# Gathered rows in three buffers and one byte per edge in a two-part graph network on one Trainium2 core

## What is computed

```
h = relu(layernorm(x))
W = einsum('rb,bio->rio', w_comp, weight)             # 16 types from 8 bases
x = x + segment_sum((h @ W[type])[src], dst) + h_bias
h = relu(layernorm(x))
h = leaky(h @ enc_w + enc_b)                          # slope 0.1
for l in range(2):
    agg = segment_sum(h[src], dst) / max(degree, 1)
    h = leaky(agg @ lin_l_w[l] + lin_l_b[l] + h @ lin_r_w[l])
x = x + h
```

## Time and profile before

| | |
|---|---|
| median of 3 runs | 3645.25 us (3639.75 to 3645.88) |
| the profiled execution | 3647.71 us, its span 3645.6 us |
| busy: PE, DVE, ACT, POOL | 66%, 82%, 52%, 68% of the span |
| setup, relational, node, layer 1 main, late | 128.7, 1102.8, 1079.8, 705.6, 628.7 us |
| share of the DMA engines in these | 0.72, 0.66, 0.90, 0.97, 0.99 |

### The profile page before, as it was taken

The page is one execution under the profiler, slowest core; times in us unless marked ns, Lnnn a source line. Parts: engine busy times, 40 slices in busy tenths (PEclk is TensorE's granted clock), DMA queues, the critical chain, the costliest instruction groups (busy, mean ns, idle before and its releaser), DMA issues. The chain is left out here.

```text
span 3645.6 us, 58608 instructions
## 1 busy us (share of the span) xinstructions
PE 2416.4 (66%) x13938; PEld 1765.4 (48%) x13938; DVE 3003.8 (82%) x8321; ACT 1899.4 (52%) x4979; POOL 2486.9 (68%) x2363
## 2 busy tenths in 40 slices
PE   0669999999999588888888888478777780000000
PEld 0435555555555366666666666377777770000000
DVE  2569999999999699999999999688898884555665
ACT  0346666666666588888888888255454550000000
POOL 0257777777777577777777777666666645676665
PEclk9989999999999899999999999799999995555555
DMA  8776667666664599999999997599999988999998
GB/s 252 295 267 194 201 208 209 208 210 211 210 202 129 194 280 281 289 287 291 290 292 290 292 295 233 201 376 380 387 389 387 379 333 347 416 416 416 415 413 329
DMA packets 664350, 1065.77 MB, mean 292 GB/s; under 512 B 74065, under 2 KB 379651, under 8 KB 657586
## 3 DMA queue, kind: packets, MB, share of 16 engines
q1 hardware_dynamic: 486572, 599.67, 50.3%
q10 hardware_dynamic: 95904, 305.70, 21.0%
q0 software_dynamic: 81536, 156.64, 13.2%
HBM read 596.92 MB, written 488.74 MB: 298 GB/s over the span
## 5 line engine op out<-in xcount | busy, mean ns | idle before, releaser
L946 PE MATMUL y_ps_rel<-w_basis,ht_rel 128*128 128x512 f32 x1568 | 754.1, 604 | 56.0 <-DVE two_rel L815 55.7
L1694 POOL DMA_INDIRECT gat_l<-base_and_means,src_c x392 | 459.0, 1171 | 211.5 <-DVE act_gat_l L1801 107.4
L1699 POOL DMA_INDIRECT means<-late_l,put_c x392 | 418.0, 1066 | 232.1 <-issue 114.4
L1084 POOL DMA_INDIRECT base_and_means<-rows_node,odd_c x392 | 423.7, 1081 | 146.3 <-issue 122.7
L668 POOL DMA_INDIRECT gat_rel<-in_x_dram,src_c x392 | 401.3, 1024 | 157.3 <-issue 81.7
L1244 ACT ACTIVATE h_node<-base_node,shift_node,rstd_node 128x128 f32<-128x128 f32 x1176 | 500.4, 483 | 1.6 <-DVE shift_node L1334 1.6
L677 POOL DMA_INDIRECT agg<-rows_rel,put_c x392 | 401.8, 1025 | 134.2 <-issue 99.9
L1075 POOL DMA_INDIRECT term_node<-agg,src_c x392 | 380.8, 971 | 128.0 <-issue 118.9
L815 DVE SCALAR_TENSOR_TENSOR two_rel<-y_ps_rel,coef,two_rel 128x128 f32<-128x128 f32 x1568 | 438.0, 341 | 0.0
L946 PEld LDWEIGHTS y_ps_rel<-w_basis,ht_rel 128*128 128x128 f32 x1568 | 265.7, 192 | 266.9 <-issue 171.2
L1624 DVE TENSOR_TENSOR last_z_l<-last_z_l,node_done_l 128x1024 f32<-128x1024 f32 x98 | 120.2, 1227 | 268.3 <-DMA node_done_l<-means 268.3
(11 more groups left out here) (167 smaller groups left out, 5993.2 us busy)
## 6 DMA issues: line engine op xcount, KB each, us to landing
pairs_l<-base_and_means SPq DMA_DIRECT2D x196, 512.0 KB, 7.7
base_and_means<-zero_row SPq DMA_DIRECT2D x49, 1024.0 KB
means<-zero_row SPq DMA_DIRECT2D x49, 1024.0 KB
first_node<-in_x_dram SPq DMA_DIRECT2D x196, 256.0 KB
term_node<-agg SPq DMA_DIRECT2D x196, 256.0 KB
x<-base_node SPq DMA_DIRECT2D x196, 256.0 KB
base_and_means<-done_node SPq DMA_DIRECT2D x196, 256.0 KB
z<-node_done_l ACTq DMA_DIRECT2D x196, 256.0 KB, 7.3
```

Of the source, the lines that this page charges most:

```text
L946: nc.tensor.matmul(y_ps[(q + j) % 2][:, c * 512:(c + 1) * 512], ht[:, q, j, :], w_basis[:, 4 * c:4 * c + 4, :], start=True, stop=True).the ...
L1084: nc.gpsimd.indirect_dma_start(pair.rearrange("n (k f) -> (n k) f", k=2), bass.IndirectOffsetOnAxis(ap=odd_c[:, t:t + 1], axis=0), rows[:, ...
L1694: nc.gpsimd.indirect_dma_start(gat[:, q, j, :], None, source, bass.IndirectOffsetOnAxis(ap=src_c[:, t:t + 1], axis=0)).then_inc(s_gathered ...
L1699: nc.gpsimd.indirect_dma_start(means1, bass.IndirectOffsetOnAxis(ap=put_c[:, t:t + 1], axis=0), rows_, None, bounds_check=N - 1, oob_is_er ...
```

## The change

1. **One byte per edge.** The setup makes `run`: for each edge 0 if its run began before its tile, else one more than its place in the tile (1 to 128). It is stored as one byte per edge in `run_d` and turned into the column `run_c`. Every pass broadcasts 896 (512) bytes into `run_b` instead of 897 (513) floats into `dst_b`: a quarter of the bytes. `select` compares `run_b` with `run_c`; `find_open` compares `run_b` with the constant 0, so it becomes a TENSOR_SCALAR with one tensor in place of a TENSOR_TENSOR with two. The setup gains one POOL iota, four DVE steps on 128x512, a fifth set of four transposes and its copy, and one store.
2. **Three buffers.** `gat` of layer 1 has RING = 3 slots, with one semaphore each; the gather of half-step m waits for the adding up of m - 3.
3. **One tile later.** In layer 1 `carry_on` is done for the tile before the present one, `to_rows` three tiles behind instead of two, `finish` four instead of three.
4. `count_needed` stands behind the first `select` and `find_open`.

```diff
+                    link(nc.vector.tensor_copy(begins[:], begins_i[:]))
+                    link(nc.vector.tensor_tensor(after_begin[:], firsts[:], begins[:], ALU.subtract))
+                    link(nc.vector.tensor_scalar(run[:], after_begin[:], 0.0, None, ALU.max))
+                    nc.vector.tensor_copy(run_b[:], run[:]).then_inc(s_run, 1)
...
-                    for k, a in enumerate(order):
+                    for k, a in enumerate(order + [run]):
+                        if k == 4:
+                            pe.wait_ge(s_run, 1)
+                            pe.wait_ge(s_col, 1)
...
-                            sp.dma_start(dst_b[:, q, :], dst_f[bass.ds(m * (HALF * P), HALF * P + 1)]
-                                         .partition_broadcast(P)).then_inc(s_dstb[q], DMA)
+                            sp.dma_start(run_b[:, q, :], run_d[bass.ds(m * (HALF * P), HALF * P)]
+                                         .partition_broadcast(P)).then_inc(s_runb[q], DMA)
...
-                                                    dst_c[:, bass.ds(m * HALF, HALF)].unsqueeze(2).to_broadcast([P, HALF, P]),
+                                                    run_c[:, bass.ds(m * HALF, HALF)].unsqueeze(2).to_broadcast([P, HALF, P]),
...
-                            nc.vector.tensor_tensor(open_[:, q, :, :], columns(q), before_.to_broadcast([P, HALF, P]),
-                                                    ALU.is_equal).then_inc(s_open, 1)
+                            nc.vector.tensor_scalar(open_[:, q, :, :], columns(q), 0.0, None, ALU.is_equal).then_inc(s_open, 1)
...
-                gat = buf("gat", [P, 2, HALF, WIDE])
+                RING = 3
+                gat = buf("gat", [P, RING, HALF, WIDE])
...
-                            q, t = m % 2, m * HALF + j
-                            if m >= 2:
-                                if not l:
-                                    pool.wait_ge(s_summed, tile(m - 2, j))
-                                elif j == 0:
-                                    pool.wait_ge(s_mixed, m - 1)
+                            g, t = m % RING, m * HALF + j
+                            if m >= RING and j == 0:
+                                pool.wait_ge(s_mixed, m - RING + 1)
...
-                                carry_on(m, q, j)
+                                ago(m, q, i, j, 1, carry_on)
...
-                                ago(m, q, i, j, 3, finish)
+                                ago(m, q, i, j, 4, finish)
...
-                                ago(m, q, i, j, 2, to_rows)
+                                ago(m, q, i, j, 3, to_rows)
```

More of the change, by code:

```diff
@@ L24 @@
 I32 = mybir.dt.int32
+U8 = mybir.dt.uint8
 ALU = mybir.AluOpType
@@ L133, in gnn_kernel @@
         dst_c = sb("dst_c", [P, T])
+        run_c = sb("run_c", [P, T])
         src_c = sb("src_c", [P, T], I32)
@@ L393, in gnn_kernel @@
             src_r, kept = row("src_r"), row("kept")
+            begins_i, begins = row("begins_i", I32), row("begins")
+            after_begin, run, run_b = row("after_begin"), row("run"), row("run_b", U8)
             carry = st.enter_context(nc.sbuf_tensor("carry", [1, 2, P], F32))
@@ L583, in relational_pass @@
                 s_scattered = [[psem(f"scattered{q}{j}") for j in range(HALF)] for q in range(2)]
-                s_dstb = [psem(f"dst_b{q}") for q in range(2)]
+                s_runb = [psem(f"run_b{q}") for q in range(2)]
                 s_same, s_open = psem("same_made"), psem("open_made")
@@ L1467, in layer_pass @@
                 row_ps = [bank(f"row_ps{i}") for i in range(2)]
-                s_gathered = [[psem(f"gathered{q}{j}") for j in range(HALF)] for q in range(2)]
+                s_gathered = [psem(f"gathered{g}") for g in range(RING)]
                 s_added = [[psem(f"added{q}{j}") for j in range(HALF)] for q in range(2)]
-                s_dstb = [psem(f"dst_b{q}") for q in range(2)]
+                s_runb = [psem(f"run_b{q}") for q in range(2)]
                 s_same, s_open, s_leaked = psem("same_made"), psem("open_made"), psem("leaked")
@@ L1837, in _ @@
                         find_open(0, 0)
-                        if l:
-                            leak(0, 0)
+                        count_needed(dve)
+                        leak(0, 0)
                         steps(dve, step, 2 * span, HALVES - span, HALVES, span)
-                        if l:
-                            add_up(dve)
+                        ago(HALVES, 0, 0, 0, 1, carry_on)
+                        add_up(dve)
                     @block.scalar
@@ L1878, in _ @@
                             store(act, sweep, last, c)
-                        for j in range(3):
-                            ago(HALVES, 0, 0, j, 3, finish)
+                        for j in range(4):
+                            ago(HALVES, 0, 0, j, 4, finish)
                         if l:
@@ L1923, in _ @@
                         product(pe, sweep, walks - 1, sweep.walk - 1)
-                        ago(HALVES, 0, 0, 0, 2, to_rows)
-                        ago(HALVES, 0, 0, 1, 2, to_rows)
+                        for j in range(3):
+                            ago(HALVES, 0, 0, j, 3, to_rows)
             clear(held)
```

80 lines of the change are left out of this document (39 added, 41 removed).

## The result

| | before | after |
|---|---|---|
| median (4 runs each) | 3645.57 us (3639.75 to 3653.01) | 3547.83 us (3543.37 to 3550.01) |
| ratio, with its 95% interval | | 0.9733 (0.9715 to 0.9751) |
| the profiled execution, its span | 3647.71, 3645.6 us | 3548.38, 3546.5 us |
| setup | 128.7 | 125.4 |
| relational pass | 1102.8 | 1109.4 |

The kernel is 98 us faster. The forecast was 3567 us: inside its range, but 19 us too slow, and the stages do not fit one by one. The node pass gained 26.3 us where 19 stood, layer 1 gained 77.7 us where 56 stood, and the relational pass took 6.6 us more where 3 less stood.

A forecast was written before the change was run, and what follows sets the result against it. It took POOL to bound the relational pass, DVE the node pass, DVE's chain and transfers together layer 1, transfers the late part. From 3647.7 us profiled, -3 - 19 - 56 = -78 gave 3570, or 3567 us as median; range 3528 to 3616.

The forecast's parts named there:

- rival A: Layer 1: DVE sets the pace at 10.5 us per half-step, node pass gains 26 us; 3532 us in all, chance 0.18.
- Layer 1, -56 us predicted: Layer 1: half-step falls from 12.03 to 11.02 us, where the transfers become the limit; -56 us, ends -7 and -84.
- The DMA engines thus work 1.02 / 1.03 of 12.03 = 11.9 us per half-step: Layer 1: DMA share against the late part's full share read as transfers needing 11.9 us, just under DVE's chain.
- The other half of the term: Layer 1: without 1.1 us of waits for PE and 0.46 us of find_open, DVE needs 10.5 us per half-step.
- Node pass, -19 predicted: Node pass: DVE's beat falls by 0.264 us, of which 0.19 us per beat is saved; -19 us, bounds 0 and -26.
- DVE at 10.36 leaves POOL, with 10.2 of its own, only 0.16 us of hold-up per beat: Node pass: POOL, held up some 0.4 us per beat now, would with 0.26 make a beat of 10.46 us.
- Rival C: Node pass: POOL's hold-ups do not shrink and its beat stays at 10.6 us; 3586 us in all, chance 0.12.
- Relational pass, -3 predicted: Relational pass: POOL sets the pace, so a shorter find_open only eases its hold-up; -3 us, between -11 and +5.
- rival D: All find_open: one-tensor instructions and POOL transfers exclude each other, +24 us relational, +41 node; 3654 us, chance 0.05.
- No cost: Setup steps, the place of count_needed: edits priced at nothing, setup 3 us if uncovered; late part untouched at 629 us.
- Rivals B and E: B: short packets keep layer 1 at 11.9 us, 3616 us, 0.12; E: broadcasts unfavourable, find_open costs the same, 3640 us, 0.03.

The follow-up runs named there:

- lag_only: The kernel before with only carry, row products and evictions of layer 1 one tile later; 3612.01 us, ratio 0.9900.
- bytes_only: The changed kernel with two gather buffers and the old lags in layer 1, leaving the byte per edge and the place of count_needed; 3594.81 us, ratio 0.9849.
- floats: The changed kernel with the place in the tile stored and broadcast as a four-byte float again; 3595.74 us, ratio 0.9848.
- all_two: The changed kernel with find_open as a two-tensor instruction again in all passes; 3600.50 us, ratio 0.9861.
- the last run: The changed kernel with layer 1's find_open and loads of pairs cut and six gathers for seven, on a chip where the kernel before took 4429 us; 10.52 us per half-step.

## Why the prediction was right, and where it was not

The total lay in the range, but the sum behind it was not the right one. 3547.8 us is nearer to rival A's 3532 (16 us off) than to the forecast's 3567 (19 us off). In layer 1 and the node pass together the forecast was 29 us too small, and the relational pass made up 10 of them by being slower instead of faster. That the total came within 0.6% is in this part luck.

**Layer 1, -56 us predicted, -77.7 measured.** The step that failed is "The DMA engines thus work 1.02 / 1.03 of 12.03 = 11.9 us per half-step". A share is time in which packets are under way, and here that time grew with the length of the half-step: for the same bytes it was 1.02 x 12.00 = 12.24 us per half-step before, and 1.03 x 11.35 = 11.69 in lag_only. With bytes it was 1.01 x 11.48 = 11.6 in bytes_only and 1.03 x 10.58 = 10.9 in the changed kernel. The true need with floats was 11.34 (lag_only, floats), hence the transfers allowed 10.58 or less where the prediction had 11.0. The witness of room was in the earlier trace rows: 385 GB/s against 416 in the late part at nearly the same share. The prediction used the two shares and not the two throughputs.

The other half of the term was right nearly to the digit. DVE's waits were 1.1 us per half-step (12.00 - 10.95 by all_two's row), `find_open` gave 0.46, and DVE's row came to 10.49 where 10.5 stood. This is rival A, for layer 1 and, by its full 26 us, for the node pass. One reading beside it was off: by the earlier trace rows a gather took 375.21 / 330 = 1.14 us, with 0.30 of issue, so that seven took 10.1 us of 12 and not 9. POOL could still afford its waits, but it lay closer behind DVE than was written, and in the changed kernel its seven make 10.5 us.

The parts do not add up: bytes alone give 29 us in this stage, lags alone 36, both (with the buffer) 78. DVE's row and waits lay above the transfers' 11.34 by 0.66, so the lags alone ran into them, and only the bytes opened the rest. The bytes and the shorter `find_open` together are worth 0.52 us as long as DVE waits for PE; the bytes alone, with the shorter `find_open` in both, are worth 0.76 us (floats against the changed kernel, 41.5 us of the stage) once it does not.

**Node pass, -19 predicted, -26.3 measured.** DVE gave the full 0.26 us and POOL followed. The step that failed here is "DVE at 10.36 leaves POOL, with 10.2 of its own, only 0.16 us of hold-up per beat": it took POOL's hold-ups as its own. They shrank with DVE's beat instead, 4 x 0.059 = 0.24 us per beat in the scatters alone. Line L1084 before and L1099 after (count, busy us, mean ns, idle before):

```profile
L1084 POOL DMA_INDIRECT base_and_means<-rows_node,odd_c x392 | 423.7, 1081 | 146.3 <-issue 122.7 <-DVE rows_node L1389 23.6
```

```profile
L1099 POOL DMA_INDIRECT base_and_means<-rows_node,odd_c x392 | 400.7, 1022 | 144.6 <-issue 120.7 <-DVE rows_node L1401 23.9
```

Rival C, a beat that stays at 10.6, falls with the 10.36 measured.

**Relational pass, -3 predicted, +6.6 in this pair of profiles.** Over thirteen kernels the pass took 1102.6 to 1113.1 us. The three with the old comparisons lie at 1102.8, 1106.7 and 1104.7, the ten with the new ones at 1108.0 in the mean. So the pair overstates it, and a loss of 3 us lies within the spread of 5 either way. The mean length of POOL's scatter instructions makes a small loss probable: 1025 to 1027 ns in the three, 1046 to 1077 in the ten, while the gathers went from 1023 to 1032 ns to 1004 to 1020. The one-tensor instruction is not its cause (all_two has the longest scatters), nor is the byte (floats has 1062 ns). So rival D, which put 24 us on this pass, falls. What the ten share that lengthens a scatter remains open.

**No cost.** The setup took 119.5 to 128.8 us without the new steps and 120.0 to 128.7 with them, so they cost less than this scatter shows. The late part took 627 to 635 us in all kernels. Rivals B and E fall with 0.62 us for `find_open` and with floats against the changed kernel.

**The count.** With -26 and -78 and the rest at nothing the sum would be -104; the two profiled spans differ by 99.1, the medians by 97.7.

## What to carry to other kernels

A DMA share near 1 does not say that transfers set the pace; compare the throughput with the best that the same kernel reaches elsewhere, and look who waits for a transfer. When an engine's row of instructions has gaps that end with a product just begun, ask for it one tile later: here that cost nothing that showed and was the larger half. Price a change by the limit that comes next after each part, since two parts that each stop at the other's limit are worth more together than apart.

## What the runs showed of the hardware

A comparison of 128x512 elements with one tensor took 416 ns on floats and 418 on bytes, on ACT as an activation 712 ns; 128x896 took 620 ns on DVE and 1.04 us on ACT.

The share of the DMA engines read 1.01 at 370 GB/s, 1.02 at 385, 1.03 at 403 and at 416. In this range it hardly tells one pace from another.

An instruction of DVE and a transfer instruction of POOL do touch each other. Between 200 and 1150 us of the relational pass, the gathers that overlap `find_open` took 1.26 us on average in the changed kernel (34 of them) and the others 1.00. But in the kernel before, beside the instruction with two tensors, they took 1.11 (50 of them) against 1.01, so this is no matter of the one-tensor form alone, and a longer gather is also likelier to overlap. The Trainium skill, "SBUF — State Buffer", section "Who interferes with whom", makes the two-port kind the strict one, an exclusive lock for a whole instruction. The gathers lean that way, but the price did not show in the pace: with two tensors (all_two) the pass took 1111.7 us and not less.

The small rows show the touch from the other side. In the changed kernel's trace a 128x7 instruction of DVE (`var_rel`, 172 ns at the median) that starts 0.54 to 0.73 us after POOL began a transfer instruction ends 0.95 or 1.01 us after that beginning, so it takes 234 to 411 ns; 11 of 56 do. Those that start within the first 0.47 us of a transfer, or after 0.83 us, keep to their usual time.

In the last run the node pass, the same code as in the changed kernel, took 1530 us in place of 1054. A stretch of it:

```profile
1600.00:2400.00 800.00, 563.50 (x3077) 436.54 (x3075) 535.11 (x1663) 481.62 (x1095) 416.29 (x416) 0.85 0.63 187
```

The granted clock there is 0.85 in the mean where it was 1.00, and no engine is busy more than 71%. What else was different on that chip the trace does not show.
